# Half of the layer-norm passes moved to GpSimd, and the squaring of the next tile issued before the statistics arithmetic

## The reference

```python
x = x + layernorm(attn(layernorm(x)))     # causal attention with rope; Wq, Wk, Wv, Wo
x = x + layernorm(ffn(layernorm(x)))      # silu(x@Wg.T * gs) * (x@Wu.T * us), then @Wd.T * ds; inner size 5632
def layernorm(x): return (x - mean(x)) / sqrt(var(x) + 1e-5)
```

## Time and profile before

| | us |
|---|---|
| median of 2 runs | 4299.78 (4297.28 to 4302.27) |
| profiled execution | 4305.27 |
| its span, slowest core | 4303.6 |
| spans of the eight cores | 4266.3 to 4303.6 |

### The profile page before, as it was taken

How to read it: one execution, slowest core, us unless ns; L and a number is a source line. 1 busy time by engine, 2 the same in 40 slices (tenths; PEclk the granted TensorE clock), 3 DMA queues, 4 the chain that set the end, 5 groups by cost and what they waited for, 6 DMA issues and landing times.

```text
span 4303.6 us, 34297 instructions; the slowest of 8 cores (4266.3 to 4303.6 us)
## 1 busy us (share of the span) xinstructions
PE 3130.0 (73%) x12212; PEld 1161.9 (27%) x12448; DVE 1345.1 (31%) x1249; ACT 738.3 (17%) x780; POOL 404.6 (9%) x287
## 2 busy tenths in 40 slices
PE   5663578988888856777778776723888888788870
PEld 1110234443433322111111112201333333333320
DVE  2665515645545446222222220063000000000012
ACT  2221000000000000444444441122000000000000
POOL 0000000000000000333333330000000000000004
PEclk9776789999999978888888888955999999988985
DMA  5553931011111162011111103222333333243323
GB/s 167 160 165 96 168 72 59 34 58 54 54 57 54 53 107 79 22 33 36 38 40 40 40 10 82 36 78 67 61 59 59 59 61 67 59 84 57 57 38 117
DMA packets 183206, 294.32 MB, mean 68 GB/s; under 512 B 6656, under 2 KB 121344, under 8 KB 180864
## 3 DMA queue, kind: packets, MB, share of 16 engines
q0 software_dynamic: 44352, 102.77, 14.6%
q1 hardware_dynamic: 138688, 189.34, 14.1%
HBM read 323.54 MB, written 71.30 MB: 92 GB/s over the span
## 4 chain that ended last, share of the span: by engine, by line
PE 64%; DVE 14%; ACT 8%; DMA 6%; issue 3%; POOL 2%; another core or an unknown queue 2%; POOLq 0%; ACTq 0%; DVEq 0%; SPq 0%
PE psA L159 22%; PE psB L159 20%; PE psD L159 8%; PE psC L159 7%; PE psE L159 6%; ACT esb L547 2%; DVE lno L271 2%; DVE lno L273 2%; DMA lns<-ln_scr 2%; POOL esb L557 2%; DVE hdn L737 1%; ACT gt L734 1%; ACT xsq L229 1%; DMA xa<-xctx 1%
## 5 line engine op out<-in xcount | busy, mean ns | idle before, releaser
L159 PE MATMUL psA<-h,gsb 128*128 128x512 bf16 x1380 | 330.9, 398 | 159.6 <-DVE hdn L737 127.7
L159 PE MATMUL psA<-lns,wk_sb 128*128 128x512 bf16 x1004 | 243.3, 401 | 155.5 <-DMA lns<-ln_scr 84.5
L557 POOL TENSOR_TENSOR esb<-esb,mask_sb 128x1024 bf16<-128x1024 bf16 x128 | 271.0, 2117 | 808.4 <-ACT esb L547 808.4
L159 PE MATMUL psB<-h,usb 128*128 128x512 bf16 x1379 | 309.2, 379 | 1.5
L557 DVE TENSOR_TENSOR esb<-esb,mask_sb 128x1024 bf16<-128x1024 bf16 x128 | 105.0, 820 | 571.5 <-ACT esb L547 571.5
L737 DVE SCALAR_TENSOR_TENSOR hdn<-psB,us_sb,gt 128x1024 bf16<-128x1024 f32 x44 | 56.5, 1284 | 721.6 <-ACT gt L734 721.6
L159 PE MATMUL psC<-wv_sb,lns 128*128 128x512 bf16 x1005 | 233.9, 383 | 13.3 <-DMA wv_sb<-wv 12.4
L159 PE MATMUL psE<-esb,ones_c 128*1 128x512 bf16 x768 | 243.5, 400 | 0.0
L159 PE MATMUL psD<-wv_sb,lns 128*128 128x512 bf16 x1003 | 235.1, 385 | 11.0 <-DMA wv_sb<-wv 9.9
L159 PE MATMUL psD<-esb,vsb 128*128 128x512 bf16 x499 | 156.8, 395 | 113.3 <-POOL esb L557 80.3
L159 PEld LDWEIGHTS psA<-h,gsb 128*128 128x128 bf16 x1408 | 139.8, 101 | 351.8 <-issue 208.4
(11 more groups left out here) (154 smaller groups left out, 3170.2 us busy)
## 6 DMA issues: line engine op xcount, KB each, us to landing
xa<-xctx SPq DMA_DIRECT2D x8, 4096.0 KB, 25.0
gsb<-wg POOLq DMA_DIRECT2D x44, 512.0 KB, 5.1
usb<-wu POOLq DMA_DIRECT2D x44, 512.0 KB, 7.1
dsb<-wd POOLq DMA_DIRECT2D x32, 704.0 KB, 6.4
ln_scr<-lno SPq DMA_DIRECT2D x10, 2048.0 KB, 10.8
lns<-ln_scr SPq DMA_DIRECT2D x8, 2048.0 KB, 10.5
k_scr<-kout SPq DMA_DIRECT2D x128, 128.0 KB, 1.9
v_scr<-vout SPq DMA_DIRECT2D x32, 512.0 KB, 2.6
```

The costliest lines, as they stand in the source:

```text
L159: en.matmul(o, l, r, start=a, stop=z))
L557: en.tensor_mul(b[:], b[:], m)))
```

## The change

Two edits in stage 1. The norm passes of odd tiles go to GpSimd, those of even tiles stay on VectorE. In the loop, `s_prep(i)` is emitted ahead of `math(i-1)`, so that on ScalarE the Square of tile i stands ahead of the square root of tile i-1. On TensorE and SP the order of instructions is what it was; on VectorE only the odd norms are gone from the row. The waits of the norm (for the copies, and for the store of the tile before) go with it to GpSimd; the store and the next copies wait on GpSimd's semaphore for odd tiles.

```diff
--- before.py
+++ after.py
@@ -263,7 +263,7 @@
                     p.wt("s", *norm[j - 1])
                 p.dat("s", lambda en: en.copy(rbc[:], psC[:]))
                 cp_tgt[j] = p.dat("s", lambda en: en.copy(bbc[:], psD[:]))
-                eng = "v"
+                eng = "v" if j % 2 == 0 else "g"
                 p.wt(eng, sS, cp_tgt[j])
                 srcb = xa[j % 4]
                 if j >= 1:
@@ -285,9 +285,9 @@
                 lds[i] = p.dma("y", f"xa{i % 4}", lambda en, s=srch, b=xa[i % 4]: en.dma_start(out=b[:], in_=s))
                 if i >= 2:
                     finish(i - 2)
+                s_prep(i)
                 if i >= 1:
                     math(i - 1)
-                s_prep(i)
             finish(8)
             math(9)
             finish(9)
```

## The result

The changed kernel takes 4338.9 us (median), the kernel before 4301.2 on the same chips; the ratio is 1.008, 95% interval 1.0059 to 1.0100, thus 25 to 43 us slower, and within 2%. The medians are of all executions, the ratio only of those in which no die's cores were slowed by a lower granted clock. The forecast was 4327 us, 27 slower, in a range of 4312 to 4344.

What follows compares the result with a forecast made beforehand. Stage 1 was taken as bound by the load loop, 79.9 us per two tiles instead of 75.1; losses of 7.7 up to M(1), 14.4 over three pairs and 5.0 at the end make 27.1, giving 4327 us, range 4312 to 4344.

Steps and rivals of the forecast that it cites:

- The load loop: Stage 1, odd tiles: store j, load j+3, its sums, spread and norm of j+2; 79.9 us per two tiles.
- the store of the one `lno`: Stage 1, odd mark to even norm: the norm waits for the odd tile's store, 11.0 us.
- Landing, sums and spread to the norm's start: Part of the load loop in stage 1: norm of j+2 can't start before 48.2 us after store j's issue.
- Price of the GpSimd norm: Odd tiles in stage 1: two GpSimd passes with their gap, taken as 31.7 us.
- The upper bound from the attention rows: GpSimd norm priced per element from short attention passes: 17.0 us a pass, 34.1 for two.
- The sum: Stage 1 marks added up to the last store: 446.3 us against 419.2, a loss of 27.1 us.
- M(1): Stage 1: M(j) is when SP issues the store of tile j; M(1) was forecast at 132.9 us.
- The hold of L253: Even tiles, stage 1: VectorE's L253 held 14 us by GpSimd's second pass, priced at nothing; as deciding rival 0.07.
- GpSimd slower on two float32 inputs: Rival on odd norms in stage 1: 17.0 us a pass instead of 15.8, 12 us more, 4339; chance 0.15.
- The early load: Rival in stage 1: sums start by M + 19.3 instead of 25.5, pairs 73.7 us, total 4308; chance 0.08.
- The later stages: From stage 2 on: assumed to keep their time; the rival that they don't was allowed 5 us either way.
- The aside that the edits pull apart: Stage 1: new order alone, all norms on VectorE, gives M(9) = 381.5, 38 us less; moving odd norms loses that and 27 more.

Runs made afterwards that it cites:

- experiment 3: Changed kernel (both edits) with each load issued one store earlier, load j+4 behind store j; ratio 1.0025 to the kernel before.
- experiment 6: Kernel before with loads one store earlier, norm passes placed behind the next tile's statistics arithmetic, and the offset rounded to bf16; ratio 0.9734.
- experiment 2: Kernel before with only the odd norms moved to GpSimd, old order kept; ratio 1.008.
- experiment 8: Changed kernel with loads one store earlier, two `lno` buffers, two pairs of `rbc` and `bbc`, a single `xsq`; ratio 0.9954 to the kernel before.

## Why the prediction held, and where it was off

*What ended last: right.* The load loop was named as the bound of odd tiles, and the store of the one `lno` as that of even ones. The waits in the changed profile say the same, and experiment 3 takes the loop away and gets the 75.4 computed with the measured price. Landing, sums and spread to the norm's start were put at 48.2 us (the terms add up to 48.1); they are 49.6, 48.0 and 50.6, as the loads land in 24.7 to 26.2 us and the 48 sums take 18.7 to 19.9.

*Price of the GpSimd norm: the mis-sized term.* 31.7 us was taken, and the rows were read as showing that the type makes no difference. Each of them had exactly one float32 input (in the first two `rbc` or `bbc`), so they could not show it; the same holds for VectorE's 8693 and 8692 ns, whose pass takes 4.43 us with none (experiment 6). The norm is 33.4 us (33.3 to 34.0). That the first pass differs from the second (17.5 against 15.8) was named as a sign of being wrong, and it came. Ten passes lie in series, five of them on the missing price, 5 x 1.76 = 8.8 us. The upper bound from the attention rows, 17.0 per pass, was exceeded by the first pass (17.5) and not reached by the second; as a sum it held, 33.4 against 34.1. By the Trainium skill, "GPSIMD Engine Reference", section "Elementwise — side-by-side cycle accounting", a float32 pass would be an estimated 18.0 us; for the pass with two float32 inputs that was nearer than the rows I trusted.

*The sum.* The stage is 10.5 us longer than added up, so the weights of stage 2 are asked for at 465.6 instead of about 455. M(1) 135.1 against 132.9; three pairs 249.5 against 239.7; the last two tiles 72.1 against 73.7. Of 10.5 us too little at M(9), 8.8 are the pass and 4.7 a later M(0), longer loads and stretched second passes, less 3.0 at M(8): the store of tile 7 has no load beside it and landed in 7.75 us, not 10.8. I had held that as a bound only, though the row of the last store shows it.

*The hold of L253: right in kind, and seen to cost next to nothing.* In the timeline of the changed kernel:

```profile
202.42 0.68 DVE L253 SCALAR_TENSOR_TENSOR st_b<-st_m,st_r 1x512 f32<-1x512 f32 x1
202.46 16.27 POOL L273 TENSOR_TENSOR lno<-lno,bbc 128x8192 bf16<-128x8192 bf16 x1
229.95 8.69 DVE L271 TENSOR_TENSOR lno<-xa,rbc 128x8192 bf16<-128x8192 f32 x1 [26.85 <-DMA ln_scr<-lno]
...
284.42 15.78 POOL L273 TENSOR_TENSOR lno<-lno,bbc 128x8192 bf16<-128x8192 bf16 x1
284.85 15.90 DVE L253 SCALAR_TENSOR_TENSOR st_b<-st_m,st_r 1x512 f32<-1x512 f32 x1
311.65 8.69 DVE L271 TENSOR_TENSOR lno<-xa,rbc 128x8192 bf16<-128x8192 f32 x1 [10.91 <-DMA ln_scr<-lno]
```

Tile 4's L253 slips into the gap between GpSimd's passes; tile 6's starts in the second pass and lasts 15.90 us, to 300.75, 0.55 behind GpSimd's end. Tile 2's lasts 7.44 us and tile 8's 1.52, each until 0.54 or 0.55 behind the end of a pass; a hold of 14 us for all was forecast. Yet the norms of tiles 4 and 6 start alike behind the mark before them, at 218.81 + 11.1 and 300.27 + 11.4, both waiting for the store. The other side was not in my sum: GpSimd waits too. The pass at 202.46 lasts 16.27 us instead of 15.76; L253 was under way when it began. So it was in four of the five second passes of experiment 2, which last 16.04 or 16.05, while the fifth takes 15.76. Together that is under 1 us over the stage. With a second `lno` about 5 us a pair was priced for L253; in experiment 8 it is 6.0, and the hold of the norm's first pass, 11.6, was not foreseen.

*The rivals.* "GpSimd slower on two float32 inputs" is what the case is, at 8.8 us instead of the 12 given. The early load (sums by M + 19.3) did not come: they start 25.6 to 27.1 us behind the mark. The later stages kept their time on the median of the cores; on the slowest core they differ by 11.8 us, more than the 5 allowed.

*The aside that the edits pull apart: right in sign and order.* The new order alone was put at a last store of 381.5; it is 389.8, a gain of 29 us instead of 38. That the old order with GpSimd would be as slow as both edits stood in no step of the prediction.

## What to carry to other kernels

Before work is moved to a second engine, list what keeps it in line with the work left behind: a single output buffer, a single scratch pair, an in-order queue, instructions of one engine that are held while the other's run. Here all four did, so a pass of twice the length lay on the path at full length, while issuing the loads earlier, taking the arithmetic off VectorE's path and giving the second pass a bf16 offset (4.4 instead of 8.7 us, at the price of a rounded offset) made the kernel 2.7% faster on one engine. And where an order is changed, work out the second-longest loop as well: what is gained ends there.

## What the runs showed of the hardware that was not expected

- GpSimd's two-input pass of 8192 elements takes 15.7 to 15.8 us with one float32 input and 17.5 us with two (none: not run at this size). VectorE's takes 8.69 us with one or two and 4.43 with none.
- An instruction of VectorE on one single partition (L253, 512 elements) is held to the end of GpSimd's pass like one on 128: 15.90 us in the row above. Held time is counted as busy: VectorE's L253 rows of experiment 2 have a mean of 5.94 us, where 0.68 is the work.
- A load's time to landing is no bound on the rate: with a median of 26 us to land, experiment 6 moves a tile's load and store every 25.0 us on average (marks 88.23 to 213.29, five steps).
